# Two biases of a deformable-convolution block: added by VectorE instead of by TensorE matmuls of one row of ones

## The chip, the cores and the metric

The kernel runs on one core of one Trainium2 chip. The metric is the device time of one execution in microseconds. The core has TensorE (PE, with its weight loads as PEld), VectorE (DVE), ScalarE (ACT), GpSimd (POOL) and SyncE (SP), which issues most DMAs.

## The reference, cut to what matters

The input is eight images of 56x56 places with 128 channels, in fp32 throughout. Layer 0 samples each image at learned places (a deformable 3x3 convolution in four groups) and mixes the result; an MLP follows. Layer 1 is an additive attention over all 3136 places of an image and a mixture of 64 experts.

```
xp = x @ w_in + b_in
offset, mask = from a depthwise convolution, gelu, two matmuls, softmax
y = dcn_core(xp, offset, mask) @ w_out + b_out        # b_out: the bias of the mixing
x = x + gamma1 * layer_norm(y, ln1_g, ln1_b)
m = gelu(x @ w_fc1 + b_fc1) @ w_fc2 + b_fc2           # b_fc2: the bias of the MLP's second layer
x = x + gamma2 * layer_norm(m, ln2_g, ln2_b)
t = _ln_t(x);  f, g = t @ W1[:h], t @ W1[h:]
scores[i, j] = sum_a w2[a] * tanh(f[i, a] + g[j, a] + b1[a]) + b2
x = x + (exp(scores) * lower_triangle, normalised) @ t
x = x + experts chosen by top-8 of softmax over the places
```

## The kernel before, in words

An image is cut into 25 blocks of 128 places (the last has 64) and into 49 half blocks of 64. For each half block GpSimd issues 18 indirect DMAs (L1189), which gather the four neighbours of every sampling place into one of four slots of `pool_mem`. These 18 are called a burst here; an image has 49 bursts, 882 gathers. VectorE's step `sample` (L1372 six times, then L1375) multiplies a slot by the corner weights and sums it into `y`; that frees the slot, and GpSimd may fill it again (the gather of half block t waits for `sample` of the slot's last user, nearly always t-4).

For each block a chain of steps goes to and fro over one PSUM bank, `chain_ps`:

- `turn`: PE transposes `y` (L1746), DVE copies (L1381).
- `mix`: PE multiplies by `w_out` (L1799 is the bias row, L1803 the product), DVE does the LayerNorm and adds the residual (`add_norm`: L1250, L1252, the Newton steps L1238 to L1245, L1268, L1269; then L1388).
- `turn_mid`: PE transposes, DVE copies (L1394).
- `hidden`: PE (L1814), gelu on ACT (L1663).
- `mlp_out`: PE (L1820 is the bias row, L1822 the product), DVE does a LayerNorm with `add_norm`, L1401, then a second normalisation up to L1404.
- `turn_norm` (DVE L1410) and `keys` (PE L1831, L1832; DVE L1417 to L1420).

The attention of a block follows: `unit` is a tanh on ACT (L1677, 800 per image), `score` the PE matmuls that sum it (L1846), `exp` on ACT (L1687), `values` (PE L1746 and L1875, DVE L1441), `finish` (DVE L1453 to L1461), `route` and `logits` (DVE L1467, L1473). Beside that run the steps of the next image (`image_in`, `project_in`, `patches`, `conv`, `offsets`, `weights`), which share another PSUM bank.

Every engine executes its steps in a fixed order. `list_schedule` works it out once from due times (`due_times`), needs (`needs`) and a table of durations (`LASTS`): on each engine the step that is able to run and has the earliest due time goes next. An engine whose next step waits lets nothing pass. The steady order is a loop over pairs of images; the first and last images have orders of their own, from the same table. The bias row of a matmul is a product of `ones` (1x128) and `rows` (1x256) with one row to sum over, `start=True`; the product proper accumulates onto it.

Of the kernel before, what the change touches and what calls it, by code (L numbers as in the profile page):

```python
# [7 lines left out]
ALU = mybir.AluOpType  # L8
# [4 lines left out]
P = 128  # L13
C = 128
# [20 lines left out]
HID = 512  # L35
# [128 lines left out]
def last_user(t):  # L164
# [31 lines left out]
    ("pe", "image_in"): .7, ("pe", "project_in"): 1.9, ("pe", "patches"): .7, ("pe", "conv"): 9.0, ("pe", "offsets"): 1.8,  # L196
    ("pe", "turn"): .35, ("pe", "mix"): 1.2, ("pe", "turn_mid"): .35, ("pe", "hidden"): 1.9, ("pe", "mlp_out"): 1.7,
    ("pe", "turn_norm"): .35, ("pe", "keys"): .9, ("pe", "route"): .35, ("pe", "logits"): .45,
    ("dve", "image_in"): .7, ("dve", "project_in"): .7, ("dve", "patches"): .8, ("dve", "offsets"): 4.7, ("dve", "weights"): 3.0,
    ("dve", "sample"): 6.0, ("dve", "turn"): .35, ("dve", "mix"): 3.5, ("dve", "turn_mid"): .35, ("dve", "mlp_out"): 6.7,  # L200
    ("dve", "turn_norm"): .35, ("dve", "keys"): 1.1, ("dve", "mask"): .35, ("dve", "finish"): 3.9, ("dve", "route"): .4, ("dve", "logits"): .4,
# [488 lines left out]
def network(nc, io, x2_d, xln2_d, logits_d, patches_d, chosen_d, expert_d, out, images):  # L690
    with ExitStack() as ctx:
        def sb(name, shape, dt=F32):
            return ctx.enter_context(nc.sbuf_tensor(name, shape, dt))
# [24 lines left out]
        w_fc2 = sb("w_fc2", [P, HID // P, C])  # L718
        rows = sb("rows", [1, 2 * C])
        b_hid = sb("b_hid", [P, HID // P])  # L720
        ones = sb("ones", [1, P])
        affine = sb("affine", [P, 6, C])
# [480 lines left out]
        def _(dve):  # L1203
# [12 lines left out]
            v.memset(xp_flat[:], 0.0)  # L1216
            v.memset(ones[:], 1.0)
            v.memset(y[:], 0.0)
# [29 lines left out]
            def moments(src, r):  # L1248

                v.bn_stats(bst[:r], src)  # L1250
                settle()
                v.bn_aggr(mv[:r], bst[:r])  # L1252
                settle()
                rsqrt(mv[:r, 1:2], r)
# [10 lines left out]
            def add_norm(src, out, residual, s, r):  # L1265

                moments(src, r)
                v.scalar_tensor_tensor(ln_a[:r], src, mv[:r, 0:1], affine[:r, s], ALU.subtract, ALU.mult)  # L1268
                v.tensor_tensor(ln_b[:r], residual, affine[:r, s + 1], ALU.add)  # L1269
                settle()  # L1270
# [439 lines left out]
        def _(pe):  # L1710
# [37 lines left out]
            def task(n, odd, name):  # L1748
# [47 lines left out]
                elif what == "mix":  # L1796
                    r = blk_rows(i)
                    wait(y_copied, n, i)
                    last = mm(chain_ps[:r, :C], ones[:, :r], rows[:, :C], start=True, stop=False)  # L1799
                    for s in range(r // SUB):  # L1800
                        part = slice(s * SUB, (s + 1) * SUB)
                        for half in range(2):
                            last = mm(chain_ps[part, :C], chainT[part, half * SUB:(half + 1) * SUB], w_out[part, half],  # L1803
                                      start=False, stop=half == 1)
                    last.then_inc(mixed.sem, 1)
# [11 lines left out]
                elif what == "mlp_out":  # L1817
                    r = blk_rows(i)
                    wait(gelu_done, n, i)
                    mm(chain_ps[:r, :C], ones[:, :r], rows[:, C:], start=True, stop=False)  # L1820
                    for c in range(HID // P):
                        last = mm(chain_ps[:r, :C], hid[:, c, :r], w_fc2[:, c], start=False, stop=c == HID // P - 1)  # L1822
                    last.then_inc(mlp_done.sem, 1)
# [223 lines left out]
def layout(inputs):  # L2047
# [14 lines left out]
    for r in range(4):  # L2062
# [23 lines left out]
        "w_fc2": f("L0_conv_w_fc2").reshape(HID // P, P, C).transpose(1, 0, 2),  # L2086
        "rows": np.concatenate([f("L0_conv_b_out"), f("L0_conv_b_fc2")])[None],
        "b_hid": f("L0_conv_b_fc1").reshape(HID // P, P).T,
# [39 lines left out]
```

## Time and profile before

| what | value |
|---|---|
| time, median of 3 runs | 15282.85 us (15266.24 to 15287.42) |
| time of the profiled execution | 15399.26 us |
| its span | 15397.4 us |
| TensorE clock granted, mean | 0.697 of full speed |
| PE, PEld busy | 7675.1, 3859.4 us |
| DVE, ACT, POOL busy | 5935.6, 6773.1, 6700.8 us |

No engine is busy for more than half of the span. An fp32 matmul of the program shows as two records of PE and two of PEld in the trace (the 200 bias rows of L1799 stand as x400), a transpose as one. Ends of matmuls are modelled in the profile; where the record of a reader on another engine stands much later than the modelled end, the reader's start is the surer mark of when the result was there. "remote" and "another core or an unknown queue" are how the profile names a wait whose release it could not find.

### The profile page before, as it was taken

Reading aid. Unit: us, or ns where it says so; the run is one execution under the profiler, and the core shown is the slowest. Engines: PE = TensorE matmul, PEld = TensorE weight load, DVE = VectorE, ACT = ScalarE, POOL = GpSimd, SP = SyncE. Lnnn points to the kernel's source line nnn. Section 1 sums busy time; section 2 is a strip of 40 time slices with the busy share of each in tenths; the row PEclk is TensorE's granted clock in tenths of the full one; section 3 lists DMA queues with packets and bytes.
Section 4 is the critical chain, followed back from the end, with each engine's and each line's share of the span. In section 5 each row is a group of like instructions: output and inputs, shape, how many; then the busy total and the mean of one; then the engine's idle time right before and its main releaser. Section 6 shows DMA issues by size and latency. Waiting matters only on the chain.

```text
span 15397.4 us, 152662 instructions
## 1 busy us (share of the span) xinstructions
PE 7675.1 (50%) x45913; PEld 3859.4 (25%) x45913; DVE 5935.6 (39%) x17381; ACT 6773.1 (44%) x8210; POOL 6700.8 (44%) x7060
## 2 busy tenths in 40 slices
PE   3344554455534555445554455444654445544467
PEld 2122222222222222222222222222222222222234
DVE  3333334333343334333334333443333433343343
ACT  1234642455424554245533455334553355523455
POOL 4444444444444344444444444444444444444430
PEclk6566776677766776667766777666776677766778
DMA  2111111111111111111111111111111111212324
GB/s 61 45 46 34 31 42 44 45 33 34 40 46 41 31 36 42 47 39 32 38 40 46 39 32 37 43 46 37 31 40 41 48 35 33 57 55 62 94 69 158
DMA packets 453794, 711.94 MB, mean 46 GB/s; under 512 B 146561, under 2 KB 260994, under 8 KB 451330
## 3 DMA queue, kind: packets, MB, share of 16 engines
q0 software_dynamic: 225792, 462.87, 11.3%
q1 hardware_dynamic: 227170, 239.11, 4.9%
q8 instruction: 384, 6.29, 0.2%
q14 instruction: 448, 3.67, 0.1%
HBM read 595.45 MB, written 105.96 MB: 46 GB/s over the span
## 4 chain that ended last, share of the span: by engine, by line
another core or an unknown queue 36%; ACT 16%; PE 16%; issue 14%; DVE 12%; DVEq 5%; DMA 1%; SPq 0%; POOL 0%; ACTq 0%; POOLq 0%
ACT tanh L1677 13%; PE score_ps L1846 7%; DVEq L1208 5%; DVE pool_mem L1372 2%; PE value_ps L1875 2%; DVE newton L1243 2%; PE side_ps L1777 1%; DVE rstd L1245 1%; PE turn_ps L1746 1%; PE chain_ps L1814 1%; ACT expo L1687 1%; DVE bst L1250 1%; ACT L1687 1%; PE chain_ps L1822 1%
## 5 line engine op out<-in xcount | busy, mean ns | idle before, releaser
L1677 ACT ACTIVATE tanh<-key_rep,query 128x896 f32<-128x896 f32 (+7 forms) x6400 | 5560.0, 950 | 5834.7 <-remote 3382.9
L1189 POOL DMA_INDIRECT pool_mem<-patches_even,pool_mem x3528 | 3350.3, 950 | 4142.1 <-DVE y L1375 3038.2
L1189 POOL DMA_INDIRECT pool_mem<-patches_odd,pool_mem x3528 | 3350.3, 950 | 4124.9 <-DVE y L1375 3100.9
L1846 PE MATMUL score_ps<-tanh,score_w 128*32 128x512 f32 (+3 forms) x24320 | 3703.9, 650 | 2566.8 <-ACT tanh L1677 1562.2
L1846 PEld LDWEIGHTS score_ps<-tanh,score_w 128*32 128x32 f32 x24320 | 855.6, 126 | 4803.6 <-issue 2891.3
L1875 PE MATMUL value_ps<-values,expoT 128*128 128x129 f32 (+1 forms) x5200 | 1019.9, 346 | 301.0 <-issue 194.6
L1372 DVE TENSOR_TENSOR pool_mem<-pool_mem 128x384 f32<-128x384 f32 x2352 | 1136.1, 552 | 47.7 <-issue 45.5
L1375 DVE TENSOR_REDUCE y<-pool_mem 128x64 f32<-128x2304 f32 x392 | 1000.9, 2553 | 36.0 <-issue 6.7
L1875 PEld LDWEIGHTS value_ps<-values,expoT 128*128 128x128 f32 (+1 forms) x5200 | 898.6, 249 | 423.2 <-issue 300.9
L1441 DVE COPY expoT<-turn_ps 128x512 f32<-128x512 f32 (+4 forms) x800 | 456.9, 572 | 1214.5 <-remote 829.0
L1746 PE MATMUL turn_ps<-ident,expo 128*128 128x128 f32 (+1 forms) x2632 | 572.9, 341 | 682.6 <-DVE expoT L1441 510.4
L1687 ACT ACTIVATE expo<-score_ps,tiny 128x896 f32<-128x896 f32 (+9 forms) x416 | 383.4, 922 | 897.1 <-remote 599.8
L1243 DVE SCALAR_TENSOR_TENSOR newton<-rstd,newton 128x1 f32<-128x1 f32 (+1 forms) x2403 | 528.3, 220 | 211.4 <-issue 34.9
L1746 PEld LDWEIGHTS turn_ps<-ident,expo 128*128 128x128 f32 (+1 forms) x2632 | 393.8, 178 | 822.9 <-DVE expoT L1441 452.5
L1250 DVE BATCH_NORM_STATS2 bst<-chain_ps 128x6 f32<-128x128 f32 (+1 forms) x400 | 118.3, 296 | 1231.6 <-remote 721.2
L1814 PE MATMUL chain_ps<-chainT,w_fc 128*128 128x128 f32 (+1 forms) x1600 | 338.6, 379 | 501.1 <-DVE chainT L1394 418.8
L1687 ACT ACT_TABLE_LOAD x197 | 252.8, 1283 | 760.1 <-remote 686.3
L1831 PE MATMUL chain_ps<-chainT,w_key 128*128 128x128 f32 (+1 forms) x400 | 140.4, 450 | 843.5 <-DVE chainT L1410 563.8
L1777 PE MATMUL side_ps<-pool_mem,early 128*128 128x448 f32 x1008 | 427.5, 581 | 108.1 <-DVEq L1208 107.0
L1245 DVE SCALAR_TENSOR_TENSOR rstd<-newton,rstd 128x1 f32<-128x1 f32 (+1 forms) x2403 | 385.7, 161 | 222.0 <-issue 31.8
L1394 DVE COPY chainT<-chain_ps 128x128 f32<-128x128 f32 (+1 forms) x200 | 57.3, 287 | 1070.0 <-remote 894.4
L1814 PEld LDWEIGHTS chain_ps<-chainT,w_fc 128*128 128x128 f32 x1600 | 300.8, 280 | 599.2 <-DVE chainT L1394 459.9
(170 smaller groups left out, 6557.5 us busy)
## 6 DMA issues: line engine op xcount, KB each, us to landing
pool_mem<-in_weight SPq DMA_DIRECT2D x64, 1024.0 KB, 9.1
pool_mem<-patches_even,pool_mem POOLq DMA_INDIRECT x3528
pool_mem<-patches_odd,pool_mem POOLq DMA_INDIRECT x3528
patches_even<-pool_mem SPq DMA_DIRECT2D x104, 256.0 KB, 2.0
patches_odd<-pool_mem SPq DMA_DIRECT2D x104, 256.0 KB
pool_mem<-in_x SPq DMA_DIRECT2D x56, 224.0 KB
x_tok<-in_x SPq DMA_DIRECT2D x192, 64.0 KB
x_d<-x SPq DMA_DIRECT2D x192, 64.0 KB
```

Of the source, the lines that this page charges most:

```text
L1189: pool.indirect_dma_start(gathered[:, b, j * 4 * CG:(j + 1) * 4 * CG], None, patches_flat[int(odd)], bass.IndirectOffsetOnAxis(ap=index[:, ...
L1208: return v.drain()
L1243: v.scalar_tensor_tensor(newton[:r, 1:2], rstd[:r], rstd[:r], newton[:r, 0:1], ALU.mult, ALU.mult)
L1372: v.tensor_tensor(part, part, weight[:, lo:lo + PIECE].unsqueeze(2) .to_broadcast([P, PIECE, CG, 4]), ALU.mult)
L1375: v.tensor_reduce(y[:, i // 2 % 2, b].rearrange("p (g c) -> p g c", c=CG), product.rearrange("p (g t) c k -> p g c t k", g=2), AX_XY, ALU. ...
L1677: nc.scalar.activation(tanh[:, ui % TANH_SLOTS, :w], key_rep[:, lo:lo + w], ACT.Tanh, bias=query[:, col:col + 1]).then_inc(tanh_done.sem, 1)
L1687: nc.scalar.activation(expo[:r, ci % 2, :w], score_ps[:r, ci % 2, :w], ACT.Exp, bias=tiny[:r, 2:3])\
L1746: return mm(out, src, ident[:r, :r], is_transpose=True, start=True, stop=True)
L1777: last = mm(side_ps[:, :BAND], taps[:, t], x_pad[:, i * BAND_ROWS + dy:(i + 1) * BAND_ROWS + dy, dx:dx + W], start=t == 0, stop=t == TAPS - 1)
L1814: last = mm(chain_ps[:, c * P:c * P + r], w_fc1[:, c * P:(c + 1) * P], chainT[:, :r], start=True, stop=True)
L1846: last = mm(score_ps[32 * col:32 * col + 32, ci % 2, lo:hi], score_w[:, place], tanh[:, ui % TANH_SLOTS, lo:hi], start=place == 0, stop=pl ...
L1875: last = mm(value_ps[:r, :C + 1], expoT[:wj, pi % 2, z, :r], values[:wj, value_place(odd, j)], start=j == 0, stop=j == k)
```

## The change

VectorE adds the bias: `add_norm` begins with a tensor_tensor that reads `chain_ps` and a row of `rows` and writes a new tile `biased` in SBUF; the statistics and the first scalar_tensor_tensor then read `biased`. The two matmuls of one row are gone, the first product proper has `start=True`. `rows` is now replicated over 128 partitions by the host's layout, `ones` and its memset are gone, and PE posts a semaphore of its own (`pe_step`) ahead of the matmuls of `mix`. The table of durations is changed to match, and so the orders come out differently.

```diff
@@ LASTS
-    ("pe", "turn"): .35, ("pe", "mix"): 1.2, ("pe", "turn_mid"): .35, ("pe", "hidden"): 1.9, ("pe", "mlp_out"): 1.7,
+    ("pe", "turn"): .35, ("pe", "mix"): .9, ("pe", "turn_mid"): .35, ("pe", "hidden"): 1.9, ("pe", "mlp_out"): 1.4,
-    ("dve", "sample"): 6.0, ("dve", "turn"): .35, ("dve", "mix"): 3.5, ("dve", "turn_mid"): .35, ("dve", "mlp_out"): 6.7,
+    ("dve", "sample"): 6.0, ("dve", "turn"): .35, ("dve", "mix"): 3.9, ("dve", "turn_mid"): .35, ("dve", "mlp_out"): 7.1,
@@ tiles
-        rows = sb("rows", [1, 2 * C])
+        rows = sb("rows", [P, 2 * C])
+        biased = sb("biased", [P, C])
-        ones = sb("ones", [1, P])
@@ vector
-            v.memset(ones[:], 1.0)
             def add_norm(src, out, residual, s, r):
-                moments(src, r)
-                v.scalar_tensor_tensor(ln_a[:r], src, mv[:r, 0:1], affine[:r, s], ALU.subtract, ALU.mult)
+                v.tensor_tensor(biased[:r], src, rows[:r, s // 3 * C:(s // 3 + 1) * C], ALU.add)
+                settle()
+                moments(biased[:r], r)
+                v.scalar_tensor_tensor(ln_a[:r], biased[:r], mv[:r, 0:1], affine[:r, s], ALU.subtract, ALU.mult)
@@ tensor, mix
-                    last = mm(chain_ps[:r, :C], ones[:, :r], rows[:, :C], start=True, stop=False)
+                    nc.tensor.sem_inc(pe_step, 1)
...
-                                      start=False, stop=half == 1)
+                                      start=half == 0, stop=half == 1)
@@ tensor, mlp_out
-                    mm(chain_ps[:r, :C], ones[:, :r], rows[:, C:], start=True, stop=False)
...
-                        last = mm(chain_ps[:r, :C], hid[:, c, :r], w_fc2[:, c], start=False, stop=c == HID // P - 1)
+                        last = mm(chain_ps[:r, :C], hid[:, c, :r], w_fc2[:, c], start=c == 0, stop=c == HID // P - 1)
@@ layout
-        "rows": np.concatenate([f("L0_conv_b_out"), f("L0_conv_b_fc2")])[None],
+        "rows": np.tile(np.concatenate([f("L0_conv_b_out"), f("L0_conv_b_fc2")])[None], (P, 1)),
```

First place, TensorE in the first image, around the first block's `mix` and `mlp_out`. Before (`y`, `mid` and `hid` are the block's data, `early` and `pool_mem` the next steps of the image's front):

```order
L1746 MATMUL chain_ps<-ident,y 128x128
L1777 MATMUL side_ps<-pool_mem,early 128x448 x9
L1799 MATMUL chain_ps<-rows,ones 128x128
L1803 MATMUL chain_ps<-w_out,chainT 64x128 x4
L1788 MATMUL side_ps<-early,pool_mem 64x54 x14
L1746 MATMUL chain_ps<-ident,mid 128x128
L1777 MATMUL side_ps<-pool_mem,early 128x448 x9
L1814 MATMUL chain_ps<-chainT,w_fc1 128x128 x4
L1788 MATMUL side_ps<-early,pool_mem 64x54 x14
L1820 MATMUL chain_ps<-rows,ones 128x128
L1822 MATMUL chain_ps<-w_fc2,hid 128x128 x4
```

And now, in the same stretch of TensorE's order:

```order
L1747 MATMUL chain_ps<-ident,y 128x128
L1778 MATMUL side_ps<-pool_mem,early 128x448 x9
L1804 MATMUL chain_ps<-w_out,chainT 64x128 x4
L1789 MATMUL side_ps<-early,pool_mem 64x54 x14
L1747 MATMUL chain_ps<-ident,mid 128x128
L1778 MATMUL side_ps<-pool_mem,early 128x448 x9
L1815 MATMUL chain_ps<-chainT,w_fc1 128x128 x4
L1789 MATMUL side_ps<-early,pool_mem 64x54 x14
L1822 MATMUL chain_ps<-w_fc2,hid 128x128 x4
```

The two matmuls of `rows` and `ones` are gone and nothing else moved here. (Line numbers after the memset are one lower, after the new lines in `add_norm` one higher.)

Second place, VectorE at one `mix` of the steady loop (block 20). Before:

```order
L1381 COPY chainT<-chain_ps 128x128
L1385 REGISTER_ALU
L1250 BN_STATS bst<-chain_ps 128x6
L1252 BN_AGGR mv<-bst 128x2
L1238 TENSOR_SCALAR newton<-mv 128x1
```

And now:

```order
L1382 COPY chainT<-chain_ps 128x128
L1386 REGISTER_ALU
L1266 TENSOR_TENSOR biased<-chain_ps,rows 128x128
L1249 BN_STATS bst<-biased 128x6
L1251 BN_AGGR mv<-bst 128x2
L1237 TENSOR_SCALAR newton<-mv 128x1
```

One instruction stands ahead of the statistics, and these read SBUF instead of PSUM.

Third place, VectorE in the steady loop between `mlp_out` of block 20 and `keys` of block 20, around `sample` of half block 43 (the six products and the reduction into `y`). Before:

```order
L1404 TENSOR_SCALAR values<-x1,mv,rstd 128x128
L1263 REGISTER_ALU
L1441 COPY expoT<-turn_ps 128x512
L1410 COPY chainT<-chain_ps 128x128
L1365 REGISTER_ALU
L1372 TENSOR_TENSOR pool_mem<-pool_mem 128x384 x6
L1375 TENSOR_REDUCE y<-pool_mem 128x64
L1417 COPY key_rep<-chain_ps 128x128
L1418 SCALAR_TENSOR_TENSOR spread<-chain_ps,tiny,own_row 128x128
L1420 TENSOR_REDUCE query<-spread 128x16
```

And now (the `xln2` row is the last of `finish` of block 18):

```order
L1462 TENSOR_SCALAR xln2<-x2,mv,rstd 128x128
L1418 COPY key_rep<-chain_ps 128x128
L1419 SCALAR_TENSOR_TENSOR spread<-chain_ps,tiny,own_row 128x128
L1421 TENSOR_REDUCE query<-spread 128x16
L1366 REGISTER_ALU
L1373 TENSOR_TENSOR pool_mem<-pool_mem 128x384 x6
L1376 TENSOR_REDUCE y<-pool_mem 128x64
```

`finish` of block 18 and `keys` of block 20 stood behind this `sample` and stand ahead of it now. Taken over one image of the steady loop, 73 of VectorE's steps have changed the pair of samples between which they stand, 54 of them to an earlier one and 19 to a later one; GpSimd's order is the same.

## Rows read from the trace of the kernel before

**Rows 1.** The page's first part: busy us, share of the span, instructions.

```profile
PE 7675.1 (50%) x45913; PEld 3859.4 (25%) x45913; DVE 5935.6 (39%) x17381; ACT 6773.1 (44%) x8210; POOL 6700.8 (44%) x7060
```

**Rows 2.** Chain that ended last, long pieces of two images: start us, us, what.

```profile
4276.19 37.04 another core or an unknown queue
...
6150.67 37.01 another core or an unknown queue
```

**Rows 3.** Waits of GpSimd: us in total, times, longest us.

```profile
POOL pool_mem L1189 <- DVE y L1375: 6139.2, 350, 43.8
```

**Rows 4.** Windows: us, busy us (instructions) of each engine, PEclk, DMA share, GB/s.

```profile
7123.00:7141.00 18.00, 4.19 (x31) 1.21 (x23) 0.04 (x1) 3.17 (x4) 11.35 (x12) 0.69 0.18 47
7141.00:7155.00 14.00, 10.71 (x78) 6.18 (x78) 8.55 (x17) 13.87 (x17) 0.20 (x1) 0.82 0.02 4
...
7163.00:7180.00 17.00, 5.07 (x19) 2.98 (x13) 0.69 (x1) 0.00 (x0) 10.66 (x12) 0.60 0.19 50
7180.00:7203.00 23.00, 15.16 (x97) 7.16 (x100) 14.39 (x49) 22.49 (x29) 0.00 (x0) 0.77 0.02 7
```

**Rows 5.** Timeline of one burst: start us, us, engine, line, operation, idle before.

```profile
6399.22 1.92 PE L1846 MATMUL score_ps<-tanh,score_w 128*32 128x512 f32 x16
...
6401.07 0.33 PE L1746 MATMUL chain_ps<-ident,mid 128*128 128x128 f32 x1
...
6415.34 0.95 POOL L1189 DMA_INDIRECT pool_mem<-patches_odd,pool_mem  x1 [0.30 <-issue]
6419.65 0.29 DVE L1394 COPY chainT<-chain_ps 128x128 f32<-128x128 f32 x1 [14.06 <-remote]
...
6420.00 1.22 PE L1814 MATMUL chain_ps<-chainT,w_fc 128*128 128x128 f32 x4 [13.19 <-DVE chainT L1394]
```

**Rows 6.** Groups by line: busy us, mean ns, idle before and releasers.

```profile
L1799 PE MATMUL chain_ps<-rows,ones 1*128 1x128 f32 (+1 forms) x400 | 111.4, 363 | 113.3 <-issue 67.4 <-DVE chainT L1381 44.3
L1820 PE MATMUL chain_ps<-rows,ones 1*128 1x128 f32 (+1 forms) x400 | 106.2, 348 | 188.6 <-ACT hid L1663 183.0 <-issue 5.2
L1250 DVE BATCH_NORM_STATS2 bst<-chain_ps 128x6 f32<-128x128 f32 (+1 forms) x400 | 118.3, 296 | 1231.6 <-remote 721.2 <-PE chain_ps L1803 208.1 <-issue 155.6
L1250 DVE BATCH_NORM_STATS2 bst<-x 128x6 f32<-128x128 f32 (+1 forms) x400 | 117.7, 294 | 40.2 <-issue 2.9
L1268 DVE SCALAR_TENSOR_TENSOR ln_a<-chain_ps,mv,affine 128x128 f32<-128x128 f32 (+1 forms) x400 | 140.2, 351 | 32.9 <-issue 2.9
L1388 DVE SCALAR_TENSOR_TENSOR mid<-ln_a,rstd,ln_b 128x128 f32<-128x128 f32 (+1 forms) x200 | 70.4, 352 | 16.6 <-issue 1.7
L1269 DVE TENSOR_TENSOR ln_b<-x_tok,affine 128x128 f32<-128x128 f32 (+1 forms) x200 | 56.4, 282 | 0.0
```

**Rows 7.** Timeline at one `mix` and one `mlp_out`, TensorE.

```profile
6014.94 0.48 PE L1799 MATMUL chain_ps<-rows,ones 1*128 1x128 f32 x2
6015.35 0.66 PE L1803 MATMUL chain_ps<-w_out,chainT 64*64 64x128 f32 x8
...
6048.02 0.48 PE L1820 MATMUL chain_ps<-rows,ones 1*128 1x128 f32 x2
6048.43 1.16 PE L1822 MATMUL chain_ps<-w_fc,hid 128*128 128x128 f32 x8
```

**Rows 8.** Timeline of VectorE's statistics at one `mix`.

```profile
6195.34 0.30 DVE L1250 BATCH_NORM_STATS2 bst<-chain_ps 128x6 f32<-128x128 f32 x1 [0.90 <-PE chain_ps L1803]
6195.71 0.18 DVE L1252 BATCH_NORM_AGGREGATE mv<-bst 128x2 f32<-128x6 f32 x1
```

**Rows 9.** Shares of the chain that ended last, by line.

```profile
by line: another core or an unknown queue 35.8%; issue 14.4%; ACT tanh L1677 13.4%; PE score_ps L1846 6.9%; DVEq L1208 4.8%; DVE pool_mem L1372 2.4%; PE value_ps L1875 1.9%; DVE newton L1243 1.7%; PE side_ps L1777 1.3%; DVE rstd L1245 1.3%; 
```

**Rows 10.** Group of VectorE's Newton products, columns as in rows 6.

```profile
L1243 DVE SCALAR_TENSOR_TENSOR newton<-rstd,newton 128x1 f32<-128x1 f32 (+1 forms) x2403 | 528.3, 220 | 211.4 <-issue 34.9
```

**Rows 11.** Timeline of one `finish`, first and last instruction.

```profile
6002.51 0.16 DVE L1453 TENSOR_SCALAR den<-value_ps 128x1 f32<-128x1 f32 x1 [13.98 <-remote]
...
6006.15 0.35 DVE L1461 TENSOR_SCALAR xln<-x,mv,rstd 128x128 f32<-128x128 f32 x1
```

## Prediction

> **What bounds the kernel now.** I read the page's first part [rows 1]: no engine is busy for more than half of the span, so the question is who waits for whom. The chain that ended last names "another core or an unknown queue" for 35.8% of the span and no other line for more than ACT's 13.4% [rows 9]. Its long pieces come back image after image: one of 37 us at 4276.19, the next of its kind at 6150.67 [rows 2]. One image of the steady loop thus takes 1874.5 us, and with 49 bursts of gathers in it a burst comes every 1874.5 / 49 = 38.3 us.
>
> GpSimd's waits say what releases a burst: `sample`, 6139.2 us in 350 waits, 17.5 us each [rows 3]. Since a cycle is 38.3 us, about 21 us of it are the burst and 17.5 the wait. So the period is set by how fast VectorE gets from the end of one burst to the end of the next `sample`.
>
> The windows show what the other engines do meanwhile [rows 4]. In 18 us within one burst VectorE is busy 0.04 us, in 17 us within another ACT 0.00 us; in the stretches without gathers VectorE is busy 8.55 of 14 and 14.39 of 23 us. TensorE goes on issuing slowly in a burst (4.19 of 18 us, 31 records), but its results arrive late: the transpose of `turn_mid` has its record at 6401.07 and VectorE's copy of it starts at 6419.65, after 14.06 us of idling and 3.4 us after the end of the burst's last gather [rows 5]. So VectorE and ACT, which live on TensorE's results, stand still for some 18 us of each cycle and do their work in the other 20 us. These 20 us have no engine full either: VectorE 0.61 to 0.63, TensorE 0.66 to 0.77, ACT nearly all [rows 4]. Every step there waits for a step on another engine. What the change is worth is therefore the latency it adds or takes on the chain of a block, as far as that chain decides when `sample` ends.
>
> **What is removed from TensorE.** 200 matmuls of one row in `mix` and 200 in `mlp_out`. Busy time is 111.4 + 106.2 = 217.6 us [rows 6]. On the path the gap from start to start counts: 0.41 us (6014.94 to 6015.35) and 0.41 us (6048.02 to 6048.43) [rows 7]. 400 x 0.41 = 164 us. In `mix` a sem_inc takes the removed matmul's place. No row shows a sem_inc alone on TensorE; it costs between 0 (it only passes the sequencer) and the whole 0.41 us of the matmul, and I take 0.15, nearer the lower end, since it moves no data. Net for TensorE: 200 x 0.26 + 200 x 0.41 = 134 us.
>
> **What is added to VectorE.** 400 tensor_tensors of 128x128 from PSUM. The trace has no such instruction. Its neighbours are the SBUF one of L1269, 282 ns, and the two-operand scalar_tensor_tensor out of PSUM, 351 ns [rows 6]. I take 290 ns, nearest to the same operation. Behind it stands a settle; the statistics show what such a pair costs beyond the instruction: 0.30 us of L1250, but 0.37 us from its start to that of L1252 [rows 8]. So 0.37 us each, between 0.34 and 0.45: 400 x 0.37 = 148 us, bounds 136 to 180.
>
> **Statistics and first product out of SBUF.** bn_stats takes 296 ns out of PSUM and 294 out of SBUF; the scalar_tensor_tensor 351 from PSUM and 352 from SBUF [rows 6]. Worth 0, within 400 x 0.003 = 1 us. The Trainium skill (Perfetto Trace Analysis, section Optimizing Scalar/DVE Operations) gives about 60 ns of access overhead for VectorE on SBUF and about 125 on PSUM; by that each of 800 instructions would be 65 ns shorter, an estimate of 52 us of busy time given back. The pairs of groups in rows 6 contradict it, and the sum goes by them.
>
> **How much of either lies on the path.** For VectorE's norm chain the chain that ended last tells: L1243 is 1.7% of it, 0.017 x 15397 = 262 us [rows 9], of 528.3 us in all [rows 10], so one half. The other half is done while VectorE would have waited anyway. `mix` and `mlp_out` of TensorE stand directly ahead of these norms in the same block, so I take the same half. VectorE: +0.5 x 148 = +74 us. TensorE: -0.5 x 134 = -67 us. Sum: +7 us. At the ends of both prices it is 68 - 82 = -14 and 90 - 41 = +49 us.
>
> **The rest.** The load of `rows` grows from one partition to 128, the memset of `ones` goes: each once, in the prologue, under 1 us. `chain_ps` comes free no earlier for the product of the next step, because the next step (`turn_mid`, `turn_norm`) needs the whole norm. ACT's work is unchanged.
>
> **The order.** The table of durations differs by 0.3 to 0.4 us in four entries, and 73 of VectorE's steps per image change the pair of samples between which they stand, 54 to earlier places, 19 to later; GpSimd's order is the same. Where a step that needs TensorE gets ahead of `sample`, the burst waits for it: at `sample` 43 `finish` 18 (4.0 us from L1453 to the end of L1461 [rows 11]) and `keys` 20 now stand ahead. Each step moved earlier in one cycle is gone from a later one, so over 49 cycles the work sums to zero; only idle time made or saved by the move counts, and its bounds are both signs. One whole 4.0 us in each of the seven cycles into which a `finish` moves is 28 us per image, 8 x 28 = 224 us, as a gain or a loss. I take 0.
>
> **Sum.** 15399 + 7 = 15406 us for the profiled execution. This stands 0.76% above the median of 15282.85; a sum of +7 us on the median gives 15290 us.
>
> **Rivals.**
> *Faster: the dropped matmuls are dear in a burst.* In the four windows, 31 + 19 of 225 records fall into stalled stretches of 35 us, 0.70 us each, and there TensorE gives out one result after another with nothing beside it [rows 4]. If the removed 800 records lie like the others, 800 x 0.22 x 0.70 = 124 us go at full value, and the rest at half, 0.78 x 67 = 52 us: -124 - 52 + 74 = -102 us. Time 15283 - 102 = 15180. For it: TensorE still runs in bursts, so chain steps are among its records. Against it: VectorE sees results only behind the burst [rows 5], so a record saved inside may bring nothing.
>
> *Slower: the order delays samples.* TensorE-bound steps now ahead of `sample` (43 is the place looked at) hold up the gathers. If in the seven cycles into which a `finish` moves `sample` comes 4 us later, 224 us are lost; if a good third of it is made up in the cycles that the steps left, since others of these are held by something else, about 140 us stay: 15420. For it: a cycle has only 20 us for work. Against: each step moved leaves its room elsewhere. It decides once more than one cycle of an image loses 4 us net (8 x 4 = 32 us).
>
> *Slower: VectorE pays all, TensorE nothing.* If the product behind a bias matmul had to wait anyway, as for its weights, TensorE's saving is nil, and if VectorE's norms lie wholly on the path its 148 us stand in full: 15283 + 148 = 15430. Against it: the bias matmul of `mlp_out` itself waits for gelu's `hid`, 183.0 of its 188.6 us of idle time [rows 6], and the product follows at once behind it [rows 7], so its going must bring the product forward.
>
> *No change at all.* If bursts set the pace so that block chains have slack everywhere, both terms are 0: 15283. The wait of 17.5 us per burst [rows 3] speaks against it, though the time would be like that of my forecast.
>
> **Chances.** Terms cancel, order averages out (with the no-change case): 0.50, own range 15210 to 15350. Dear matmuls: 0.20. Order delays: 0.20. VectorE pays all: 0.10. The likeliest gives 15290; the range, to leave out no more than 2 in 10, goes from 15110 (dear matmuls and a gain of the order together) to 15430. A measurement here tells 0.2% from no change, 31 us, so the band of "same" is 15252 to 15313. Of the first case 0.26 falls into it; the other 0.24 are gains and losses of the order, 0.16 on the faster side, since 54 moves are to earlier places, and 0.08 on the slower. Faster: 0.16 + 0.20 = 0.36. Slower: 0.08 + 0.20 + 0.10 = 0.38.
>
> **What the changed profile would show.** The new tensor_tensor at about 290 ns x400 and VectorE busy about 5936 + 400 x 0.29 = 6052 us. L1249 and L1269 (out of SBUF) at 295 and 352 ns: if they are 60 ns shorter, my weighing of that rule was wrong. TensorE busy about 7675 - 218 = 7457 us. The gap from the copy of `turn` to the first product of `mix` would show the sem_inc. The period between the long pieces of the chain: 1873 to 1876 us by the forecast, near 1862 by dear matmuls, near 1892 by delayed samples. GpSimd's wait for `sample` moves with it: 6139 by the forecast, about 6040 and 6280 by the two rivals. The forecast is wrong if the period moves by over 10 us, and its step on the order is wrong if it moves while the norm chain's share and the PE prices come out as said.

## The result and the profile after

| | before | after |
|---|---|---|
| median | 15285.14 us (15266.24 to 15292.49, 4 runs) | 15139.98 us (15122.33 to 15154.41, 4 runs) |
| ratio | | 0.9905 (95% interval 0.989 to 0.9919) |
| span of the profiled execution | 15397.4 us | 15152.6 us |

The kernel is 145 us faster, 0.95%. The forecast was 15290 us, no change. (The profiled execution of before lies 0.76% above its median, so the 245 us between the two spans overstate the change.)

The page's first part of after, columns as in [rows 1]:

```profile
PE 7392.2 (49%) x45113; PEld 3712.8 (25%) x45113; DVE 6055.5 (40%) x17780; ACT 6766.0 (45%) x8210; POOL 6690.9 (44%) x7060
```

VectorE has 120 us more of work, as foreseen (6052 us). TensorE has 283 us less, where 218 were foreseen. The groups of after that answer to [rows 6]:

```profile
L1266 DVE TENSOR_TENSOR biased<-chain_ps,rows 128x128 f32<-128x128 f32 (+1 forms) x400 | 115.3, 288 | 1234.4 <-remote 880.4 <-PE chain_ps L1804 151.3 <-PE chain_ps L1822 140.6
L1249 DVE BATCH_NORM_STATS2 bst<-biased 128x6 f32<-128x128 f32 (+1 forms) x400 | 117.7, 294 | 33.0 <-issue 3.5
L1269 DVE SCALAR_TENSOR_TENSOR ln_a<-biased,mv,affine 128x128 f32<-128x128 f32 (+1 forms) x400 | 140.6, 351 | 33.3 <-issue 3.5
```

The addition takes 288 ns (290 were taken). The statistics and the product now read SBUF and take 294 and 351 ns, where [rows 6] had 296 and 351 out of PSUM. The idle time ahead of the norm, 1231.6 us before, is 1234.4 us ahead of the addition.

The long pieces of the chain, for [rows 2], and the first of GpSimd's waits, for [rows 3]:

```profile
7432.51 37.77 another core or an unknown queue
...
9282.88 37.76 another core or an unknown queue
```

```profile
POOL pool_mem L1189 <- DVE y L1376: 5904.7, 349, 37.5
```

A steady image takes 1850.4 us instead of 1874.5, and GpSimd waits 235 us less for `sample`. The prediction had put 1862 us and 6040 us for the rival "dear matmuls". The two drops, of the image and of the wait, lean on the profiled execution of before, which lies high, so only their direction counts. The stall itself is as it was: in these 38 us VectorE is busy 0.29 us.

```profile
7432.00:7470.00 38.00, 5.32 (x32) 3.81 (x32) 0.29 (x1) 6.12 (x6) 24.52 (x26) 0.53 0.18 47
```

Now the place that the prediction had looked at, `sample` 43, with `finish` 18 and `keys` 20 moved ahead of it. These are the reductions of `sample` 42, 43 and 44 of one steady image, first before, then after:

```profile
7333.88 2.55 DVE L1375 TENSOR_REDUCE y<-pool_mem 128x64 f32<-128x2304 f32 x1
...
7366.15 2.55 DVE L1375 TENSOR_REDUCE y<-pool_mem 128x64 f32<-128x2304 f32 x1
...
7407.75 2.55 DVE L1375 TENSOR_REDUCE y<-pool_mem 128x64 f32<-128x2304 f32 x1
```

```profile
7186.03 2.55 DVE L1376 TENSOR_REDUCE y<-pool_mem 128x64 f32<-128x2304 f32 x1
...
7223.12 2.55 DVE L1376 TENSOR_REDUCE y<-pool_mem 128x64 f32<-128x2304 f32 x1
...
7257.90 2.55 DVE L1376 TENSOR_REDUCE y<-pool_mem 128x64 f32<-128x2304 f32 x1
```

Before, 32.3 and 41.6 us; after, 37.1 and 34.8 us. The moved steps do hold `sample` 43 back, by 4.8 us, but the next one comes 6.8 us sooner. The two together are 2.0 us shorter. In e2 below, which has the order alone, the five steady images show the same: 37.4 and 35.0 us on average, against 32.3 and 41.7 us in the kernel before.

### The profile page after: what moved, and what is told of

Same layout as the page of the kernel before. It is cut to its first block, busy times and chain, and to the rows that moved or that the text cites. A ratio compares the mean times of both kernels' runs of the same rounds, so it can differ in the third digit from the quotient of the medians.

```text
span 15152.6 us, 152058 instructions
## 1 busy us (share of the span) xinstructions
PE 7392.2 (49%) x45113; PEld 3712.8 (25%) x45113; DVE 6055.5 (40%) x17780; ACT 6766.0 (45%) x8210; POOL 6690.9 (44%) x7060
## 4 chain that ended last, share of the span: by engine, by line
another core or an unknown queue 37%; ACT 20%; PE 13%; issue 12%; DVE 12%; DVEq 5%; DMA 1%; SPq 0%; POOL 0%; ACTq 0%; POOLq 0%
ACT tanh L1678 17%; PE score_ps L1846 6%; DVEq L1208 4%; DVE pool_mem L1373 2%; DVE newton L1242 2%; PE value_ps L1875 2%; DVE rstd L1244 1%; PE side_ps L1778 1%; DVE bst L1249 1%; ACT L1664 1%; PE turn_ps L1747 1%; ACT expo L1688 1%; ACT L1688 1%; ACT hid L1664 1%
## 5 line engine op out<-in xcount | busy, mean ns | idle before, releaser
L1189 POOL DMA_INDIRECT pool_mem<-patches_odd,pool_mem x3528 | 3346.8, 949 | 4037.8 <-DVE y L1376 3014.6
L1189 POOL DMA_INDIRECT pool_mem<-patches_even,pool_mem x3528 | 3344.0, 948 | 3988.4 <-DVE y L1376 2890.2
L1846 PE MATMUL score_ps<-tanh,score_w 128*32 128x512 f32 (+3 forms) x24320 | 3613.8, 639 | 2235.8 <-ACT tanh L1678 1285.3
L1266 DVE TENSOR_TENSOR biased<-chain_ps,rows 128x128 f32<-128x128 f32 (+1 forms) x400 | 115.3, 288 | 1234.4 <-remote 880.4
L1664 ACT ACTIVATE hid<-chain_ps,b_hid 128x128 f32<-128x128 f32 (+1 forms) x800 | 226.3, 365 | 709.8 <-remote 504.0
L1822 PE MATMUL chain_ps<-w_fc,hid 128*128 128x128 f32 (+1 forms) x1600 | 281.8, 330 | 421.2 <-ACT hid L1664 288.3
```

The source lines that it names most:

```text
L1189: pool.indirect_dma_start(gathered[:, b, j * 4 * CG:(j + 1) * 4 * CG], None, patches_flat[int(odd)], bass.IndirectOffsetOnAxis(ap=index[:, ...
L1846: last = mm(score_ps[32 * col:32 * col + 32, ci % 2, lo:hi], score_w[:, place], tanh[:, ui % TANH_SLOTS, lo:hi], start=place == 0, stop=pl ...
```

## The experiments

Each ratio is to runs of the kernel before on the same chip in the same series, which took 15281 us (e1 to e4), 15268 (e5 to e8), 15277 (f13 to f16) and 15423 (g17, g18). Runs e9 to e12 met something else and are told together. A series is a set of runs on one chip. "Old order" means that the table of durations, and with it the order of every engine, is that of before.

### The two halves of the change: e1 and e2

e1 is the changed kernel with the table of before; e2 is the kernel before with the changed table.

```diff
 # e1, in the changed kernel; e2 is the reverse, in the kernel before
-    ("pe", "mix"): .9, ("pe", "mlp_out"): 1.4, ("dve", "mix"): 3.9, ("dve", "mlp_out"): 7.1
+    ("pe", "mix"): 1.2, ("pe", "mlp_out"): 1.7, ("dve", "mix"): 3.5, ("dve", "mlp_out"): 6.7
```

> The change's arithmetic (VectorE adds the biases, no bias matmuls) with the old table of durations, so every engine's order is that of before. Theory 'order' (the 145 us gained come from the moved steps, the terms of the arithmetic cancel as predicted): 15290 us, ratio 1.000 (0.998 to 1.003), period of a steady image 1874 us. Theory 'dear matmuls' (the removed matmuls save more than predicted): 15140 us, ratio 0.990, period 1850 us.

Measured: 15209.22 us, ratio 0.9953 (0.9941 to 0.9966).

> The arithmetic of before with the new table of durations alone, so every engine's order is that of after. Theory 'order': 15140 us, ratio 0.990. Theory 'dear matmuls': 15285 us, ratio 1.000 (0.998 to 1.003).

Measured: 15198.52 us, ratio 0.9947 (0.9934 to 0.996). Neither theory holds alone. The arithmetic gives 0.47%, the order 0.53%, and 0.9953 x 0.9947 = 0.9900 agrees with the change's 0.9905 (0.989 to 0.9919). About half of the gain comes from four numbers in a table.

### The two sides of the arithmetic: e3, e4, e5

```diff
 # e3, in e1: no bias anywhere; the statistics and the first product read chain_ps again
-                v.tensor_tensor(biased[:r], src, rows[:r, ...], ALU.add)
-                settle()
 # e4, in the kernel before: the new vector code beside the bias matmuls; statistics and product read biased
+                v.tensor_tensor(biased[:r], src, affine[:r, s], ALU.add)
+                settle()
 # e5, in the kernel before, mix and mlp_out alike
+                    mm(chain_ps[:r, :C], ones[:, :r], rows[:, :C], start=True, stop=True)
                     last = mm(chain_ps[:r, :C], ones[:, :r], rows[:, :C], start=True, stop=False)
```

> Old order; the two biases are left out altogether: no bias matmuls and no addition on VectorE (the output lacks b_out and b_fc2). It prices TensorE's side alone. The prediction's terms: 67 us less than before, 15218 us, ratio 0.9956. Theory 'dear matmuls': 145 + 74 = 219 us less, 15066 us, ratio 0.986.

Measured: 15226.1 us, ratio 0.9968 (0.9955 to 0.9981).

> Old order and the kernel before, with one more tensor_tensor of chain_ps into an unused tile ahead of the statistics, 400 in all. It prices VectorE's side alone. The prediction's term: 74 us more, 15359 us, ratio 1.0048; if the norms lay wholly on the path 148 us more, ratio 1.0097; if they have slack, 15285 us.

Measured: 15285.77 us, ratio 1.0007 (0.9996 to 1.0017). The text on record is wrong in one point: the statistics and the first product do read the new tile, as in the change, so this kernel's norms have another row added to them. In its instructions and shapes it is the change's vector side.

> Before, with each of the 400 bias matmuls issued twice (the second starts afresh, so nothing else is computed). Theory 'half on the path' (leaving both out gained 54 us): the same size again, +54 to +80 us, 15350 us, ratio 1.0045. Theory 'slack' (an addition is absorbed as VectorE's was): within 15 us of 15281, ratio 1.000.

Measured: 15343.57 us, ratio 1.0052 (1.0039 to 1.0065).

TensorE's side comes out as the prediction had it: leaving the matmuls out gains 0.32%, 49 us (67 taken), and doubling them costs 0.52%, 79 us of 400 x 0.41 = 164, about half. VectorE's side does not: 148 us of new work cost 0.07%, 11 us, with an interval from -6 to +26. e1, which is e3 plus the additions, is even 17 us below it by the medians of one series. So the additions cost next to nothing in both kernels, and the parts do not add up exactly: e3 and e4 give -38 us together, e1 has -71.

Is it that the half was misread, because L1243 serves other normalisations too? Following the chain that ended last through the whole traces rules that out. In the kernel before it passes through 203 of the 400 scalar_tensor_tensors L1268, which only `add_norm` has, and in e4 through 212 of 400. The norms were half on the chain and a longer norm still cost 11 us. For TensorE the same count gives 244 of the 800 records of bias rows, 0.31 and not one half; 0.31 x 134 = 41 us is near the 49 of e3.

### VectorE elsewhere, and more of it: e6 and f14

```diff
 # e6, in the kernel before, sample
+                    v.tensor_tensor(spare[:], affine[:, 0], affine[:, 1], ALU.add)
+                    settle()
 # f14, in e1, ahead of the addition in add_norm
+                for _ in range(4):
+                    v.tensor_tensor(spare[:r], affine[:r, 0], affine[:r, 1], ALU.add)
+                    settle()
```

> Before, with one more tensor_tensor of 128x128 (about 0.29 us and its drain, 0.37 us) at the head of every sample, 392 in all; it works on a tile that nothing reads. Theory 'the end of sample sets the period': 392 x 0.37 = 145 us more, ratio 1.0095. Theory 'compensation' (a later burst gives TensorE and ScalarE as much more time ahead of the stall as VectorE lost, and these have work queued): under 30 us, ratio under 1.002.

Measured: 15343.29 us, ratio 1.0055 (1.0042 to 1.0067): 84 us of 145. Nothing could be more directly on the path than `sample`, which releases the gathers, and it costs little over half: less than the first theory said and more than the second.

> As e10: 576 us more of VectorE beside the norms than e1 (15209 us). Half on the path: 15497 us, ratio 1.014. Compensation: 15260 to 15410 us, ratio 0.999 to 1.008. On a chip where the kernel before takes 9430 us: 1.005 again.

Measured: 15353.35 us, ratio 1.0053 (1.004 to 1.0067). Against e1's 0.9953 that is 1.00%, 153 us of 576, a quarter and not a half, though the chain passes through 871 of these 1600 additions. So the price per addition is not a constant: near 0 for the first, about 0.1 us each for the next four.

### How a later step can end sooner

The trace of e1 shows it within one kernel. In two steady images the same instructions run in the same order, but `sample` 19 comes at slightly different times against the burst before it. VectorE, TensorE's transpose of the block's `y` and GpSimd, first image:

```profile
4533.85 2.55 DVE L1376 TENSOR_REDUCE y<-pool_mem 128x64 f32<-128x2304 f32 x1
...
4537.19 0.94 POOL L1189 DMA_INDIRECT pool_mem<-patches_even,pool_mem  x1 [0.57 <-issue]
...
4554.36 0.48 PE L1747 MATMUL chain_ps<-ident,y 128*128 128x128 f32 x1
...
4564.77 0.29 DVE L1382 COPY chainT<-chain_ps 128x128 f32<-128x128 f32 x1 [3.62 <-remote]
...
4592.58 2.55 DVE L1376 TENSOR_REDUCE y<-pool_mem 128x64 f32<-128x2304 f32 x1
```

The next image:

```profile
6388.14 2.55 DVE L1376 TENSOR_REDUCE y<-pool_mem 128x64 f32<-128x2304 f32 x1
6391.47 0.94 POOL L1189 DMA_INDIRECT pool_mem<-patches_odd,pool_mem  x1 [4.47 <-DVE y L1376]
...
6394.61 0.48 PE L1747 MATMUL chain_ps<-ident,y 128*128 128x128 f32 x1
6395.13 0.29 DVE L1382 COPY chainT<-chain_ps 128x128 f32<-128x128 f32 x1 [3.84 <-issue]
...
6433.76 2.55 DVE L1376 TENSOR_REDUCE y<-pool_mem 128x64 f32<-128x2304 f32 x1
```

In the first image `sample` is early: its burst follows the one before it without a pause (0.57 us at 4537.19), the stall goes on, and the copy of `turn` comes 30.9 us after the reduction's start. In the next image `sample` is late enough that GpSimd had to wait 4.47 us. With that pause TensorE's results get through; the copy comes after 7.0 us, and the next `sample` after 45.6 us instead of 58.7. Counted from the start of the burst ahead (4513.95 and 6364.59), `sample` 19 is 3.7 us later in the second image and the next one 9.5 us sooner (69.2 us against 78.6). Windows of e1, columns as in [rows 4], the first 22 us behind each of the two bursts' beginnings:

```profile
4537.00:4559.00 22.00, 2.34 (x9) 0.39 (x9) 0.00 (x0) 2.56 (x4) 16.63 (x18) 0.50 0.17 53
...
6391.00:6413.00 22.00, 7.59 (x50) 2.44 (x50) 3.69 (x16) 11.86 (x17) 16.35 (x18) 0.66 0.20 63
```

ScalarE works 2.56 of 22 us in the one and 11.86 in the other. It is no accident of two images. At `sample` 19, six images each of before, after, e1 to e6 and f14 give 54 cases. In the 39 with a pause under 2.5 us the copy comes after 29 to 32 us and the next `sample` after 56 to 61. In the 9 with a pause over 3.4 us they come after 6 to 8 and 46 to 49 us; the 6 between lie between. A few us of delay ahead of a burst can thus save more behind it. It is not so everywhere: over all places of these kernels, where a burst starts later than the same burst of other images, some 0.6 to 1.0 of the delay is still there at the next three. This is what the prediction's arithmetic had no term for, and a delay of every burst should show it.

### All bursts later: f15 and g18

```diff
 # f15, in the kernel before, gathers
                     nc.gpsimd.sem_inc(pool_step, 1)
+                    nc.gpsimd.memset(spare[:], 0.0)
+                    nc.gpsimd.drain()
                     for j in range(SAMPLES):
 # g18: the two new lines twice
```

> As e11: each of the 392 bursts starts about 3 us later (on the other chip 1163 us in all were added, 2.97 us each, all of it lost since GpSimd never waited there). On a chip where the kernel before takes 15280 us: if the start of a burst sets the period, 350 x 2.97 = +1040 us, ratio 1.068. Compensation: under half of it, ratio under 1.034.

Measured: 14959.9 us, ratio 0.9792 (0.9778 to 0.9805). It is faster, by 317 us. One wait, memset and first gather of its trace, and GpSimd's wait for `sample`:

```profile
6040.47 0.52 POOL L1188 MEMSET spare<- 128x512 f32 x1 [9.35 <-DVE y L1378]
6043.22 0.95 POOL L1192 DMA_INDIRECT pool_mem<-patches_odd,pool_mem  x1 [2.23 <-issue]
```

```profile
POOL spare L1188 <- DVE y L1378: 4607.6, 299, 39.8
```

Each burst starts 2.75 us later than its release, 392 x 2.75 = 1078 us of idling put into GpSimd, and the waits for `sample` shrink by more, from 6139.2 to 4607.6 us. By the gathers' records, the kernel before has 3.3 bursts per steady image that follow the last one within 1 us, and 1.2 with a pause of 1 to 6 us; f15 has none and 11.5. The next `sample` is also ready more often, since 299 bursts wait for it instead of 350.

Taken by place over five steady images, the cycles of f15 are 43 us per image shorter in sum, and 36 of these fall on the five cycles whose burst had less than 6 us of pause in the kernel before. The other 44 bursts are held back by some 120 us per image in all, and their cycles become 8 us shorter in sum, single ones by up to 12 us longer or shorter (the profile of before lies 14 us an image above its median). So most of the gain falls where a pause was missing, and elsewhere the delay costs little. At `sample` 19 all six images now have a pause of 2.9 to 3.1 us, and the next `sample` comes after 51 to 54 us.

> Before, with two memsets and two drains ahead of each burst, so some 5.2 us of delay where f15 had 2.75. If what counts is that TensorE's results on their way get out before the stall, most of that is had by the first 2.75 us and the rest costs: 0.98 to 1.00. If a burst can be held back for nothing as long as the other engines have work: 0.97 or less. If the start of a burst sets the period after all: above 1.02.

Measured: 15053.75 us, ratio 0.9768 (0.9752 to 0.9783). But the delay is not what the text on record took it to be. The first memset and the first gather of a burst in its trace:

```profile
6062.68 0.53 POOL L1189 MEMSET spare<- 128x512 f32 x1 [9.71 <-DVE y L1379]
...
6066.09 0.95 POOL L1193 DMA_INDIRECT pool_mem<-patches_odd,pool_mem  x1 [0.75 <-issue]
```

That is 3.41 us and not 5.2; the second memset with its drain adds 0.66 us to f15's 2.75. So g18 is nearly f15 once more, on another chip, and where a longer delay begins to cost stays open. The two kernels don't part the pause from the memset and drain that make it; that the pause counts is shown by the 54 cases above, which have neither.

### Which numbers in the table: e7, e8, f16

All three are the kernel before with other entries for `mix` and `mlp_out`: e7 has VectorE's alone raised (3.9 and 7.1), f16 raises them to 4.7 and 7.9, and e8 moves all four the other way. With TensorE's two entries lowered alone the kernel's scheduler finds no order that repeats from image to image, so there is no such kernel.

```diff
 # e7
-    ("dve", "mix"): 3.5, ("dve", "mlp_out"): 6.7
+    ("dve", "mix"): 3.9, ("dve", "mlp_out"): 7.1
```

> The arithmetic of before, with only VectorE's two entries of the table raised (3.5 to 3.9, 6.7 to 7.1); 23 of VectorE's steps per image move to an earlier cycle and 74 to a later one. Theory 'VectorE's steps came first because their real length was understated': faster as with the full table, 15200 us, ratio 0.995. Theory 'any change of the table deals a new order by chance': anywhere from 0.99 to 1.01, most likely not 0.995.

Measured: 15062.06 us, ratio 0.9872 (0.9855 to 0.9889).

> The arithmetic of before, with the four entries moved by as much the other way (TensorE 1.5 and 2.0, VectorE 3.1 and 6.3); 55 steps earlier, 43 later. Theory 'a direction of the table matters': slower by about as much, 15360 us, ratio 1.005. Theory 'a new order by chance': no relation to the sign.

Measured: 15300.4 us, ratio 1.0023 (1.0014 to 1.0033).

> The arithmetic of before, VectorE's two entries raised by 1.2 us (4.7 and 7.9) where e7 had 0.4; 11 steps per image earlier, 184 later. If the direction decides (VectorE's long norms taken for longer, so that steps that wait stand later): as fast as e7 or faster, 0.980 to 0.988. If the accident of single cycles decides: anywhere from 0.98 to 1.01.

Measured: 15031.9 us, ratio 0.9834 (0.9821 to 0.9848). The order alone is worth from -1.66% to +0.23%. The four tables (e2's among them) fit a direction in so far as the kernel is faster the longer VectorE's norms are taken to be. In e7 and f16 most of the steps that moved stand behind a `sample` now (74 and 184). The full table is against that as the reason: it moves 54 steps ahead and 19 behind, and gains too. And e7 and the full table differ in TensorE's entries alone and lie 0.75% apart, so the accident of single places is as large as the direction. Four tables don't settle it.

### Together: f13 and g17

```diff
 # f13: the changed kernel with e7's table; g17: with f16's table and f15's two lines
```

> As e9. On a chip where the kernel before takes 15280 us and if the parts add: ratio 0.9825, 15010 us; if single cycles decide anew, 0.982 to 0.992. On a chip where it takes 9430 us: 1.002 again.

Measured: 15051.63 us, ratio 0.9853 (0.9838 to 0.9868). It is faster than before and than the change, but the arithmetic adds only 0.19% to e7's order (intervals overlap), not 0.47%; the sum of the parts, 0.9825, lies outside.

> The change's arithmetic, VectorE's two entries raised to 4.7 and 7.9 (TensorE's as before), and the memset with a drain ahead of each burst (2.75 us from the memset to the first gather). If all add: 0.9834 - 0.0047 + (0.9792 - 1) = 0.958, 14635 us. If they save the same lost time: 0.975 to 0.980. On a chip where the kernel before takes 9430 us: slower, 1.12.

Measured: 15192.31 us, ratio 0.9849 (0.9833 to 0.9865). The three gains don't add: g17 is 0.8% worse than g18 in the same series, which has neither the change nor the table. That they save the same lost time would have given 0.975 to 0.980, so it doesn't explain g17 either; here one gain undoes part of another, and no run shows where. The fastest kernel by ratio is g18, hardly ahead of f15.

### A series in which the stalls were gone: e9 to e12

e9 is f13's kernel, e10 f14's, e11 f15's, and e12 the kernel before. In this series the kernel before took 9429.76 us (9423.43 to 9433.75, 15 runs), not 15280; on the same chip it took 15422.61 in a later one.

> The change's arithmetic with the table in which only VectorE's two entries are raised (the order that ran at 0.9872 with the old arithmetic). If the parts add: 0.9872 - 0.0047 = 0.9825, 15005 us, faster than before and than the change. If the knife edges of single cycles fall otherwise with other durations, anything from 0.982 to 0.992.

Measured: 9451.89 us, ratio 1.0023 (1.0014 to 1.0032).

> The change's arithmetic in the old order (15209 us), with four more tensor_tensors of 128x128 and their drains on a tile that nothing reads, ahead of the addition of each bias: 400 x 4 x 0.36 = 576 us more of VectorE. Prediction's rule (half of it on the path): +288 us, 15497. Theory 'compensation' (a delay costs only where it pushes a step over the start of a stall, and gains where it holds a burst back until TensorE's results are out): clearly under half, +50 to +200 us.

Measured: 9476.95 us, ratio 1.0049 (1.0036 to 1.0063).

> Before, with a memset of 128x512 and a drain on GpSimd between the wait for sample and the first gather of each of the 392 bursts. Bursts start later by that much (its size is read from the trace) and nothing else is longer. Theory 'the end of sample sets the period': the full delay x 350 waited bursts is lost. Theory 'compensation': much less than half is lost, or the kernel gets faster, since TensorE's results on their way get out before the stall.

Measured: 10592.83 us, ratio 1.123 (1.1215 to 1.1246).

> The kernel before once more, for a second profile of it: 15230 to 15310 us, steady images near 1860 us; the first profile (15399 us) had 1874.

Measured: 9430.23 us; the expectation failed by 38%, and that is the finding. From e12's trace, a window within a burst, the norm's first instruction for [rows 6], and GpSimd's wait for [rows 3]:

```profile
4000.00:4010.00 10.00, 9.83 (x64) 5.71 (x57) 5.31 (x20) 9.34 (x11) 7.56 (x9) 0.57 0.26 72
```

```profile
L1250 DVE BATCH_NORM_STATS2 bst<-chain_ps 128x6 f32<-128x128 f32 (+1 forms) x400 | 117.9, 295 | 462.8 <-PE chain_ps L1803 357.6 <-PE chain_ps L1822 99.0 <-issue 4.8
```

```profile
POOL pool_mem L1189 <- DVE y L1375: 6.1, 20, 0.3
```

While GpSimd gathers, VectorE and ScalarE work on, the norm waits 462.8 us instead of 1231.6 and never for a release that the profile can't find, and GpSimd hardly waits for `sample` (6.1 us in all): it gathers without a break and sets the time (its line L1189 is 62.0% of the chain). There a delay of a burst is lost in full: 1163 us in e11, 2.97 for each of 392. So the gains of the two kernels that were run both ways exist only where TensorE's results are held up during gathers: f15's pause, and e9's arithmetic and order, 1.5% faster there and 0.2% slower here. The change itself was not run in this series.

## Why the prediction was wrong

- **What bounds the kernel.** Right: the period is set by burst, late results and `sample`. GpSimd's waits and the period moved together (-235 us in all and -24 us an image).
- **Durations.** Right: 288 ns for the addition; 294 and 351 ns out of SBUF. The Trainium skill (Perfetto Trace Analysis, section Optimizing Scalar/DVE Operations) would have had these two 65 ns shorter; the trace of after, too, doesn't show it. The sem_inc in `mix` was taken at 0.15 us: the shortest gaps from the end of the copy of `turn` are 0.05 us to the bias row and 0.47 to the product before, and 0.15 to the product after, so it costs about 0.1 us.
- **TensorE's term, -67 us.** The size is right within the error: -49 us left out (e3, -29 to -69), +79 us doubled (e5). The half was borrowed from VectorE, though; on the chain stood 0.31 of these records.
- **VectorE's term, +74 us.** Wrong, and the first failed step. "The other half is done while VectorE would have waited anyway" took the half read off the chain for a price, and it is only a share of time. The price was +11 us (e4, -6 to +26), and for four times as much a quarter of the time added (f14). A chain of fixed durations can't do that: a step on it for half of the time would cost at least half when lengthened. Here durations depend on when a burst starts, and the burst is started by the very chain that was lengthened; a delay gives back much of what it takes by letting results out ahead of the stall. That this happens is shown (the 54 cases at `sample` 19, f15); that it is the whole reason for e4's 11 us is argued from it.
- **The order, 0 us.** The second failed step, and the larger: -81 us (e2). "Over 49 cycles the work sums to zero" is true of work. It had rightly said that only idle time counts, then took its middle. The rival that looked at `sample` 43 had the delay right (4.8 us against 4.0) and the repayment wrong: 6.8 us came back one cycle later.
- **The sum.** -49 + 11 - 81 = -119 us by the parts (the arithmetic as a whole, e1, gave -71, and with the order -152; why e1 is 33 us better than its parts stays open), measured -145. The rival "dear matmuls" had the size of the result almost right (15180), but not for its reason: the removed matmuls cost what was forecast. A gain by the order stood only among the chances, with 0.16 and without an amount. That the measured time lies inside the stated range is no merit of the forecast: the range reaches that far down for the dear matmuls and that unpriced gain.

## What to carry to other kernels

Where an engine's own progress starts what holds the others up (here GpSimd's gathers), a step's share of the chain is no price for lengthening it: measure by putting the operation in twice, and try a pause ahead of the disturbance before shortening anything. When a change edits a scheduler's cost table, time the new table with the old arithmetic and the old table with the new; here the four numbers were worth as much as the arithmetic, and raising two of them further (f16) was worth three times as much. Read from the trace how long an inserted delay really is: two memsets and drains gave 3.41 us where 5.2 were taken. A gain of this kind depends on stalls that can be gone another time, so see that the kernel before takes its usual time in the series that judges it.

## What the runs showed of the hardware that was not expected

- One kernel took 15232 to 15442 us in five series and 9423 to 9434 us in a sixth, and one of the chips gave 9430 us in one series and 15423 us in another. What differs in the trace is when TensorE's results are seen during GpSimd's indirect gathers: at once, or often only some 3.4 us behind the last gather ([rows 5]). By the semaphore records of five steady images, 32% of TensorE's releases come more than 3 us after the modelled end of their matmul in the kernel before, and 1% in e12. In the first 2 us of a burst most are still prompt. The pace of the gathers is nearly the same (0.95 and 0.97 us each, one every 1.25 us), and the DMA packets are the same (453794, 711.94 MB). The mean granted clock differs, 0.697 and 0.831, but a low one does not make the stall: e12's window above works at 0.57, the stalled ones of [rows 4] had 0.69 and 0.60. What holds the results up, and what changes between series, no run here shows.
- A memset of 128x512 and a drain on GpSimd ahead of each burst made the kernel 2.1% faster in the one case (f15) and 12.3% slower in the other (e11). A second memset and drain added only 0.66 us to the 2.75 of the first (g18).
- Within one execution the same steps in the same order took 45.6 or 58.7 us between two samples (e1).
